# Late merges on GpSimd and the second expert bias as 12-row products, in a fused attention and mixture-of-experts kernel

## What is computed

```python
x = x + tanh(g_xattn[0]) * cross_attention(layernorm(x), ctx)          # 16 heads of 16
x = x + tanh(g_ffn[0]) * ffn(layernorm(x))

def ffn(hidden):
    a = attention(layernorm(hidden) * ln1_w + ln1_b)  # 16 heads of 128, causal, rope, biases
    h = hidden + a
    return h + moe(layernorm(h) * ln2_w + ln2_b)

def moe(h):                                           # 1024 tokens, E = 4 experts, I = 256
    raw = softmax(h @ w_gate)
    top_vals, top_idx = top_k(raw, 2)
    w = softmax(top_vals)                             # two gates a token
    comb = zeros((t, E)).at[arange(t)[:, None], top_idx].add(w)
    hmid = gelu(einsum('td,edi->tei', h, we1) + be1)
    eout = einsum('tei,eid->ted', hmid, we2) + be2    # be2: 4 x 256, the second expert bias
    return einsum('te,ted->td', comb, eout)
```

## Time and profile before

| | us |
|---|---|
| median of 3 runs | 463.28 |
| lowest and highest run | 463.11, 465.21 |
| profiled execution | 467.53 |
| its span | 465.70 |
| granted TensorE clock over the span | 0.983 of full |

### The profile page before, as it was taken

The page is one execution under the profiler, slowest core; times in us unless marked ns, Lnnn a source line. Parts: engine busy times, 40 slices in busy tenths (PEclk is TensorE's granted clock), DMA queues, the critical chain, the costliest instruction groups (busy, mean ns, idle before and its releaser), DMA issues.

```text
span 465.7 us, 10305 instructions
## 1 busy us (share of the span) xinstructions
PE 415.1 (89%) x3135; PEld 361.4 (78%) x3150; DVE 364.4 (78%) x1124; ACT 286.3 (61%) x655; POOL 301.2 (65%) x433
## 2 busy tenths in 40 slices
PE   0477997998899899999999999999999996598994
PEld 0366876886776799899899898998998986586994
DVE  3854568677789797897798788888888877928997
ACT  3357674755235777587677677677677675375440
POOL 5898959720598487587587687677677555343551
PEclk9999999999999899999999999999999998989998
DMA  5600000200256875775865865855955655000011
GB/s 153 189 3 2 1 3 2 92 2 1 46 113 125 174 149 119 174 150 108 203 143 106 189 136 118 196 131 108 225 119 109 145 80 112 4 0 2 1 45 45
DMA packets 71795, 44.53 MB, mean 96 GB/s; under 512 B 57424, under 2 KB 60112, under 8 KB 71760
## 3 DMA queue, kind: packets, MB, share of 16 engines
q1 hardware_dynamic: 67680, 35.42, 36.1%
q10 hardware_dynamic: 4080, 8.69, 6.5%
HBM read 13.68 MB, written 1.05 MB: 32 GB/s over the span
## 4 chain that ended last, share of the span: by engine, by line
PE 68%; DVE 17%; issue 5%; ACT 4%; POOL 3%; DMA 2%; ACTq 0%; SPq 0%; DVEq 0%; POOLq 0%
PE bank L1464 36%; PE bank L1532 5%; PE bank L1582 5%; DVE yacc L1309 3%; PE bank L1531 3%; PE bank L1583 3%; DVE yacc L1318 2%; PE bank L1404 2%; PE bank L1445 2%; POOL room L523 2%; PE bank L1359 2%; PE bank L1380 2%; PE bank L1405 1%; DMA qk_room<-qk_room 1%; PE bank L1426 1%
## 5 line engine op out<-in xcount | busy, mean ns | idle before, releaser
L799 ACT ACTIVATE probs<-sm,nm 128x128 f32<-128x128 f32 (+1 forms) x128 | 57.0, 447 | 44.1 <-DVE nm L1184 43.8
L789 ACT ACTIVATE probs<-turned 128x768 uint16<-128x768 uint16 x60 | 64.7, 1078 | 18.1 <-DMA turned<-halves 16.5
L1464 PE MATMUL bank<-hH,qk_parts 128*128 128x512 f32 x240 | 75.4, 395 | 0.0
L536 POOL COPY halves<-probs 128x768 uint16<-128x768 uint16 x64 | 52.6, 822 | 33.0 <-DVE probs L1208 31.1
L523 POOL TENSOR_TENSOR room<-room,qk_room 128x512 f32<-128x512 f32 x32 | 41.2, 1290 | 35.6 <-DMA qk_room<-qk_room 30.6
L1464 PE MATMUL bank<-hL,qk_parts 128*128 128x512 f32 x120 | 57.7, 481 | 0.9 <-DVE room L1105 0.9
L1464 PEld LDWEIGHTS bank<-hH,qk_parts 128*128 128x128 f32 x240 | 45.2, 188 | 9.5
L1105 DVE SCALAR_TENSOR_TENSOR room<-bank,qk_bias,cst_sb 128x512 f32<-128x512 f32 x64 | 47.5, 742 | 0.0
L1076 DVE TENSOR_REDUCE nxm<-bank 128x2 bf16<-128x512 f32 (+1 forms) x48 | 32.8, 688 | 18.1 <-PE bank L1405 17.5
L523 POOL TENSOR_TENSOR room<-room,q_room 128x512 f32<-128x512 f32 x32 | 41.1, 1287 | 5.5 <-DMA q_room<-q_room 5.5
L684 ACT ACTIVATE probs<-bank 128x512 f32<-128x512 f32 x48 | 28.3, 595 | 25.4 <-PE bank L1421 14.4
(11 more groups left out here) (241 smaller groups left out, 1291.8 us busy)
## 6 DMA issues: line engine op xcount, KB each, us to landing
qk_room<-qk_room SPq DMA_DIRECT2D x64, 128.0 KB, 2.4
q_room<-q_room SPq DMA_DIRECT2D x64, 128.0 KB, 2.4
stg<-in_wqkv ACTq DMA_DIRECT2D x6, 768.0 KB, 5.8
stge<-in_we ACTq DMA_DIRECT2D x7, 256.0 KB, 3.1
stg<-in_wqkv SPq DMA_DIRECT2D x2, 768.0 KB, 5.2
stgo<-in_wo ACTq DMA_DIRECT2D x6, 256.0 KB, 3.4
x_sb<-in_x SPq DMA_DIRECT2D x4, 256.0 KB, 4.1
turned<-halves SPq DMA_TRANSPOSE x64, 2.8
```

Of the source, the lines that this page charges most:

```text
L536: pool.tensor_copy(halves[:, j % 2, :, :], PR[:, j % 2, 0:384].bitcast(U16).rearrange("p (n h) -> p h n", h=2)).then_inc(s["b_split"], 1)
L789: act.activation(*merged(j - 3), ACT.Copy).then_inc(s["b_merge"], 1)
L799: ins = act.activation(PR[:, q, a:e], sm[:, q, a:e], ACT.Exp, bias=nm[:, q, t:t + 1], scale=-1.0, accum_out=rs[:, q, t:t + 1])
L1464: ins = pe.matmul(outp, l, r, start=(m == 0), stop=(m == n - 1))
```

## The change

1. **Late merges.** LATE falls from NU - 4 to NU - 9: merges of units 55 to 59 are made on POOL, in step T as merge(T-3) behind split(T), and ACT no longer makes them. The merged probabilities get four slots in place of two, so that merge(u) waits for PV(u-4) and no longer PV(u-2). From step 58 on, DVE makes maxima(T+1) ahead of normalise(T). At the end DVE's and ACT's order changes a little: each o_low moves a place ahead, and second_norm's phases 4 and 5 of the first two sequences come behind the last o_low; o_high(58) stands between the last two exponentials.
2. **Hidden low parts.** hidden_low2(0) and (1) are made on DVE, behind the statistics of the second half of second_norm, and no longer on POOL.
3. **Gates.** The turns of the logits stand between the two halves of expert_out(0). DVE makes `y * g + x` (residual_form) at the start, for sequences 0 and 1 ahead of the copy of the logits' turns, for 2 and 3 later. The second gate exponential becomes a Tanh, which stands behind Gelu and GH of middle(4); the gates are multiplied by g as they are formed, so that nothing is left to multiply at the end.
4. **Second bias.** The bias goes through PE: be2 is loaded four times three times onto 12 rows in each quarter of the partitions (12 transfers of 4x256 on SP, ahead of the second weight load), POOL turns it into high and low rows by five operations in units 16 to 20 (`bias_rows`), with two small reductions on DVE for the factors. The gates are packed in the same way (high, low, high; three DVE operations), turned on PE (`pack_turn`) ahead of expert_out(2), copied to wvL's first half, and `second_bias(c)` makes four products of 12 rows for each chunk, behind middle(8) and middle(12). `add_biases` adds them from PSUM, four operations of 128x512. The 32 operations L1309, the four L1325 and the transfer of be2 to 128 rows go. SP's output waits for the last accumulation.

The diff, cut to its core:

```diff
-        PTs = probs[:, 2:4, :]
+        PTs = probs[:, 2:6, :]
...
-        LATE = NU - 4
+        LATE = NU - 9
...
+            sp.wait_ge(s["q_parts"], 2 * B)
+            for q in range(4):
+                for r in range(3):
+                    row = 32 * q + E * r
+                    sp.dma_start(be2_raw[row:row + E, :], be2).then_inc(s["d_be"], 16)
...
# POOL
-                pool.wait_ge(s["b_pv"], u - 1)
+                pool.wait_ge(s["b_pv"], u - 3)
...
+            def bias_rows(n):
+                if n == 0:
+                    ins = pool.tensor_copy(be2_high.bitcast(F32R), be2_raw)
+                if n == 1:
+                    ins = pool.tensor_tensor(be2_low, be2_raw, be2_high, ALU.subtract)
+                if n == 2:
+                    ins = pool.tensor_scalar(be2_low, be2_low, small[:, 142:143], None, ALU.mult)
+                if n == 3:
+                    ins = pool.tensor_scalar(be2_raw, be2_high, small[:, 143:144], None, ALU.mult)
+                if n == 4:
+                    ins = pool.tensor_tensor(be2_parts[:, :], be2_raw, be2_low, ALU.add)
...
+                if i == 2 and j < 5:
+                    bias_rows(j)
+                if U * i + j - 3 >= LATE:
+                    merge(U * i + j - 3)
...
-            hidden_low2(0)
-            hidden_low2(1)
...
# ACT
-                if unit(i, j, 3):
+                if unit(i, j, 3) and not (isinstance(i, int) and U * i + j - 3 >= LATE):
                     merge(i, j)
...
-            merge(NP - 1, 6)
             exponentials(NP - 1, 6)
+            o_high(NP - 1, 6)
             exponentials(NP - 1, 7)
-            o_high(NP - 1, 6)
...
+                if n == 5:
                     act.wait_ge(s["c_gdiff"], 1)
-                    act.activation(gate[:, 400:408], gate[:, 392:400], ACT.Exp).then_inc(s["c_gexp"], 1)
+                    act.activation(gate[:, 400:408], gate[:, 392:400], ACT.Tanh, scale=-0.5).then_inc(s["c_gexp"], 1)
...
# DVE
+                if isinstance(i, int) and T >= AHEAD:
+                    maxima(*divmod(T + 1, U))
...
+            second_norm(2, 0, 2)
...
+            hidden_low2(0)
+            hidden_low2(1)
...
+            def residual_form(b):
+                y = yacc[:, 2 * b:2 * b + 2, :].rearrange("p t n -> p (t n)")
+                xb = x_sb[:, 2 * b:2 * b + 2, :].rearrange("p t n -> p (t n)")
+                dve.scalar_tensor_tensor(y, y, small[:, 97:98], xb, ALU.mult, ALU.add).then_inc(s["c_res"], 1)
+            residual_form(0)
+            residual_form(1)
...
-            link(dve.tensor_scalar(Gt(248, 8), Gt(400, 8), 1.0, None, ALU.add))
-            link(dve.reciprocal(Gt(256, 8), Gt(248, 8)))
-            link(dve.tensor_tensor(Gt(264, 8), Gt(256, 8), Gt(400, 8), ALU.mult))
+            dve.tensor_scalar(Gt(256, 8), Gt(400, 8), half_g, half_g, ALU.mult, ALU.add)
+            link(dve.tensor_scalar(Gt(264, 8), Gt(400, 8), minus_half_g, half_g, ALU.mult, ALU.add))
...
+            link(dve.tensor_copy(packed[:, :, :, 0:E].bitcast(F32R), gates))
+            dve.tensor_copy(packed[:, :, :, 2 * E:3 * E], packed[:, :, :, 0:E])
+            dve.tensor_tensor(packed[:, :, :, E:2 * E].bitcast(F32R), gates, packed[:, :, :, 0:E], ALU.subtract).then_inc(s["c_pack"], 1)
...
-                        ins = dve.scalar_tensor_tensor(yacc[:, n, :], be2_rows[:, e, :], gate[:, 4 * n + e:4 * n + e + 1], yacc[:, n, :],
-                                                       ALU.mult, ALU.add)
...
-                        dve.scalar_tensor_tensor(y, y, small[:, 97:98], xb, ALU.mult, ALU.add).then_inc(s["c_fin"], 1)
...
+                    dve.tensor_tensor(y, y, bank[4 + hf][:, :], ALU.add).then_inc(s["c_badd"], 1)
...
+            accumulate(0)
+            accumulate(1)
+            dve.wait_ge(s["c_pack_pe"], 1)
+            dve.tensor_copy(gates_turned, bank[4][:, 0:256]).then_inc(s["c_gT"], 1)
+            residual_form(2)
+            residual_form(3)
+            add_biases(0)
...
# PE
+            def second_bias(c):
+                for hf in range(2):
+                    rows_ = slice(32 * (2 * c + hf), 32 * (2 * c + hf) + 3 * E)
+                    for t in range(2):
+                        ins = pe.matmul(bank[4 + hf][:, 256 * t:256 * (t + 1)], gates_turned[rows_, t * P:(t + 1) * P], be2_parts[rows_, :],
+                                        start=True, stop=True)
...
+            expert_out(0, (0,))
             pe.wait_ge(s["c_lgT"], 1)
...
+            expert_out(0, (1,))
             expert_out(1)
...
+            middle(7)
+            pack_turn()
+            expert_out(2)
+            for n in range(8, 2 * NE):
                 middle(n)
+                if n == 8:
+                    second_bias(0)
+                if n == 12:
+                    second_bias(1)
```

More of the change, by code:

```diff
@@ L592, in _ @@
             split(NP - 1, 6)
+            merge(NU - 5)
+            split(NP - 1, 7)
             merge(NU - 4)
-            split(NP - 1, 7)
             merge(NU - 3)
@@ L1192, in _ @@
             dve.wait_ge(s["yacc_init"], B)
+            by_quad = ident.rearrange("p (q w) -> p q w", q=4)
+            dve.tensor_reduce(small[:, 143:144], by_quad[:, :, 0:2 * E], AX.XY, ALU.add)
+            dve.tensor_reduce(small[:, 142:143], by_quad[:, :, 2 * E:3 * E], AX.XY, ALU.add).then_inc(s["c_half"], 1)
             def output_add(m, b):
@@ L1212, in step @@
                 q = j % 2
-                if unit(i, j, 0) and not (isinstance(i, int) and T == 0):
+                if unit(i, j, 0) and not (isinstance(i, int) and (T == 0 or T > AHEAD)):
                     maxima(i, j)
+                if isinstance(i, int) and T >= AHEAD:
+                    maxima(*divmod(T + 1, U))
                 c, g = chunk_at(j)
@@ L1252, in _, with hidden_low2 @@
             output_add(LAST + 3, 3)
-            for phase in range(6):
+            second_norm(2, 0, 2)
+            def hidden_low2(b):
+                dve.wait_ge(s["c_hH"], b + 1)
+                cut = slice(256 * b, 256 * (b + 1))
+                dve.tensor_tensor(hL[:, :, cut], h2T[:, :, cut], hH[:, :, cut].bitcast(F32), ALU.subtract).then_inc(s["c_h"], 1)
+            hidden_low2(0)
+            hidden_low2(1)
+            for phase in range(1, 6):
                 second_norm(2, phase, 2)
@@ L1296, in _, with accumulate @@
             link(dve.tensor_tensor(Gt(0, 32), Gt(120, 32), Gt(152, 32), ALU.add))
-            dve.wait_ge(s["d_be"], 16)
-            dve.wait_ge(s["b_yadd"], NU // 2)
-            for m in range(2 * E):
+            packed = nh[:, 1, :].rearrange("p (t b w) -> p b t w", t=2, w=32)
+            gates = gate[:, 0:32].rearrange("p (b t e) -> p b t e", b=B, e=E)
+            link(dve.tensor_copy(packed[:, :, :, 0:E].bitcast(F32R), gates))
+            dve.tensor_copy(packed[:, :, :, 2 * E:3 * E], packed[:, :, :, 0:E])
+            dve.tensor_tensor(packed[:, :, :, E:2 * E].bitcast(F32R), gates, packed[:, :, :, 0:E], ALU.subtract).then_inc(s["c_pack"], 1)
+            def accumulate(m):
                 c, e = divmod(m, E)
@@ L1320, in _, with add_biases @@
                     ins.then_inc(s["c_acc"], 1)
[L1321 to L1325 removed]
+            def add_biases(c):
+                dve.wait_ge(s["c_be"], c + 1)
+                for hf in range(2):
+                    b = 2 * c + hf
+                    dve.wait_ge(s["c_acc"], 2 * (E * c + 1) + hf + 1)
+                    y = yacc[:, 2 * b:2 * b + 2, :].rearrange("p t n -> p (t n)")
+                    dve.tensor_tensor(y, y, bank[4 + hf][:, :], ALU.add).then_inc(s["c_badd"], 1)
[6 more added lines that the diff above has]
+            add_biases(0)
+            accumulate(2)
+            accumulate(3)
+            accumulate(4)
+            accumulate(5)
+            add_biases(1)
+            for m in range(6, 2 * E):
+                accumulate(m)
         @block.tensor
@@ L1636, in expert_out @@
                     pe.wait_ge(s["b_yadd"], NU // 2)
-                for hf in range(2):
+                for hf in parts:
                     if m >= 2:
```

77 lines of the change are left out of this document (46 added, 31 removed).

## The result

The changed kernel is slower: 474.70 us median of 4 runs (474.07 to 475.79) against 464.25 for before beside it (4 runs, 463.11 to 465.66), a ratio of 1.023 with a 95% interval of 1.0201 to 1.026. Measured again beside 23 runs of before it was 1.0157 (1.0104 to 1.021). The mean of all eight runs of the changed kernel is 474.3 us, against 466.0 for the 61 runs of before beside the first two groups of experiments (463.1 to 469.6), so that I work with **+8.4 us**; the four runs measured again lie 8.3 above the 23 of before beside them. The forecast was +3.05, as 466.3 us. Of the runs that follow, one of before at 699.25 us and one of "Tanh earlier" at 475.06 us count as slow and are in no mean and no ratio.

What follows compares the result with a forecast made beforehand. TensorE, busy 89%, was taken to bound the kernel, with VectorE ending it 3.83 us later. Late units 2.0, second norm 0.2, early part 0, gates through end 0.85 sum to +3.05 on 463.28: 466.3 us, 8-in-10 range 461.0 to 469.8.

Steps and rivals of the forecast that it cites:

- one fall was a rival: Gates: clock falls behind PE's pause of about 2 us ahead of expert_out(2), adding 1.5: 467.8 us; chance 0.15.
- What bounds the kernel, and the frame: Whole kernel: TensorE, busy 89%, bounds it; differences added in the 467.53 us profile are put on the median 463.28.
- Late units, +2.0: 375 to 404 us: merges behind splits delay PV(55) by 2.65 us; last o_low 400.5 plus 1.5 for the clock's fall.
- my upper bound of +3.2: Late units: cost if the clock falls at both pauses, ahead of PV(58) and of PV(60).
- Second norm, +0.2: Ahead of the experts: hidden_low2(0) on VectorE ends at 405.65, two moved phases cost 0.3; between -0.3 and +0.6.
- Early part, 0: Before the late units: bias loads, five GpSimd operations and two VectorE reductions cost nothing; upper end +2.7.
- Gates, expert_out(2) at 433.3: Gates: three of eight small VectorE operations held by GpSimd; expert_out(2) at 433.3 against 430.65, between 430.0 and 435.5.
- the upper end: Gates: every product with two SBUF inputs waits for a full subtraction; expert_out(2) comes 2.2 us later than taken.
- Second bias and the end, +0.85: End: two bias blocks of 0.6 us on PE, VectorE's tail shrinks by 2.8; VectorE ends at 464.05 against 463.20.
- 28.5 us of PE: From expert_out(2) to PE's end: work taken from before, added to 433.3 with 1.2 for bias, giving 463.0.
- The rivals: Gates slip through, 0.16; late units break even, 0.22; clock falls behind gates' pause, 0.15; products or GpSimd rows cost most, 0.05.
- The last rival's 470: Bias products or rows on GpSimd cost their upper ends, +1.8 and +2.7 on top, 470 us; chance 0.05.

Runs made afterwards that it cites:

- first two groups of experiments: Follow-up kernels run beside before, each group on a different chip; before had means of 466.5 and 465.6 us there.
- Tanh earlier: Changed kernel with Tanh ahead of Gelu of middle(4), as the only move; mean of nine runs 469.3 us, ratio to before 1.0075.
- both moves with the late units of before: Changed kernel, residual forms 0 and 1 behind gate difference, Tanh ahead of middle(4)'s Gelu, late units as in before; mean 464.8 us, ratio to before 0.9979.
- Merge ahead of split: Changed kernel, residual forms 0, 1 behind gate difference, Tanh ahead of middle(4)'s Gelu, GpSimd's late merges ahead of splits; mean 463.0 us, ratio to before 0.9937.
- Order on VectorE alone: Changed kernel, residual forms 0, 1 behind gate difference, Tanh ahead of middle(4)'s Gelu, merges and ScalarE's end as before; mean 463.4 us, ratio to before 0.9947.
- two runs of before named above: Two runs of the unchanged kernel: 463.11 us with a mean granted clock of 0.998 over the span, 468.82 us with 0.983.
- both moves at the gates: Changed kernel with residual forms 0 and 1 behind the gate difference and Tanh ahead of middle(4)'s Gelu; mean 467.5 us, ratio to before 1.0013.
- one merge less: Changed kernel, residual forms 0, 1 behind gate difference, Tanh ahead of middle(4)'s Gelu, merge(55) left on ScalarE; mean 465.2 us, ratio to before 0.9982.

## Why the prediction was wrong

The direction and the places were right, the size was not: +3.05 forecast, +8.4 measured, and the range ended at 469.8. Two steps failed. In the gates the forecast let three small operations be held where four were, had Tanh end 1.0 us too early, and its sum put nothing for a fall of the clock behind either of the two pauses there (one fall was a rival). In the late units it took one fall of the clock, as before, where most profiles have two. Besides, the sum was put on a median that was too low.

- **What bounds the kernel, and the frame.** I put a sum made in one profiled execution on the median of three runs. That median, 463.28, was 2.7 us below the mean of 61 runs. This alone moves the forecast to 469.0. The profiled execution of 467.53 should have warned me: it lies outside the three runs (463.11 to 465.21), and the row with 0.91 from 140 to 160 us was to be seen.
- **Late units, +2.0.** Single events came as worked out: PV(55) 378.52 (forecast 378.6), PV(58) 388.20 (388.7), PV(60) 393.21 (393.6), last o_low 402.07 (400.5 and 1.5 for the fall). But the last o_low's +2.03 flatters the forecast: before had lost 0.8 us by PV(53) through its early fall. From PV(53) on it is 33.1 against 30.25, +2.8, and by many runs +3.6 (+2.9 by the ratio). The step that failed is the size of the clock's part: I took the fall as alike in both. The four profiles with the late units of before (before twice, the change without late units, both moves with the late units of before) have one fall each between 374 and 404 us and 29.6 to 30.3 us from PV(53) to the last o_low. Of the seven with all five merges behind the splits, two have one fall and 32.5 to 33.1 us, five have two and 33.9 to 34.8 us. So an equal fall leaves +2.8, and a second one, which my upper bound of +3.2 had allowed for, adds about 1.4. That the merges' place behind the splits is the cause was right ("Merge ahead of split"). VectorE's new order, which I gave no price of its own, is no loss ("Order on VectorE alone").
- **Second norm, +0.2.** +0.43 by the traces (first expert product 6.28 us behind the last o_low, before 5.85). hidden_low2 on VectorE takes 0.69 us, and the two moved phases put it later.
- **Early part, 0.** Nothing to be seen in the windows up to 360 us.
- **Gates, expert_out(2) at 433.3.** This is the term that failed most. The 433.3 stands in the frame of before, without the delay of the late units: 27.4 us behind the first expert product. It came 29.9 us behind it (438.26 - 408.35; before 24.8), so that the wait and the operations took 2.5 us more than forecast. The wait ahead of expert_out(1) grew by 0.7, less than I gave (1.0 to 1.5), but I priced no fall behind it, since 1.39 us had had none; behind 2.13 there was one, 1.5 us. It pushed middle(4), and Tanh stands behind middle(4)'s Gelu: Tanh ended 23.4 us behind the first expert product instead of 22.4. Then every second one of the dependent operations was held for a whole subtraction, four and not three: 5.6 us where I had 3.9. The sentence from the Trainium skill ("SBUF — State Buffer", "SBUF: two separate sides": an exclusive lock for a whole instruction) gave the upper end. The measurement agrees with the lock, four operations at 1.14 to 1.26 us beside subtractions of 1.3, none over 0.3 where GpSimd had nothing to do; but only each second operation met it, not every one, as that upper end had assumed.
- **Second bias and the end, +0.85.** The products were 0.6 us a block as taken (from the last product of middle(8) at 443.82 to the second of middle(9) at 444.92 there are 1.10 us, where two steps of 0.23 are usual). Of the 1.8 us more that the draining of "TensorEngine Tiling (Array Packing)", "Key Properties", in the Trainium skill might have cost, there is no sign. VectorE ends 0.91 behind PE (forecast 1.07). (A middle is 6 products, not 12 as the description of the kernel says; its duration in the sum came from the rows.) What failed was the 28.5 us of PE: expert_out(2) ran at half clock, +1.46. In the two profiles the forecast missed 7.38 - 3.05 = 4.3 us, and 2.5 of them lie in the gates and 1.5 here.
- **The rivals.** The fall behind the gates' pause was a rival with a chance of 0.15 and happened in every profile with that pause. I treated the rivals as excluding one another and the forecast; gates late, falls at two places and the low base came together. (The last rival's 470 is 466.3 + 1.8 + 2.7 = 470.8.) As a sum of its parts, 463.28 + 2.7 (base) + 3.6 (late) + 4.0 (gates and bias) = 473.6, it is the measured mean to within 1 us. How much of it is the clock can be estimated: the eight runs of the change have a mean granted clock of 0.982, those of before 0.990, and the two runs of before named above differ by 5.7 us for 0.015, which makes about 3 of the 8.4 us.

## What to carry to other kernels

Where an engine's queue gets extra work for a unit that is older, put it ahead of the newer unit's work: the same merges cost 3 to 4 us behind the splits and nothing that could be measured ahead of them. A chain of small dependent operations on VectorE belongs where GpSimd is idle; the same eight operations took 5.6 us beside GpSimd's subtractions and 1.55 ahead of them. And a sum that is made in one profile is to be put on a mean of many runs, with every pause that the change adds priced with the fall of the clock behind it.

## What the hardware showed that I had not expected

- At the gates the granted clock fell to 1.2 GHz for 3 to 4 us (in one profile for nearly 7) behind each pause of TensorE of 2.12 to 2.13 us (four profiles) and of 2.93 to 2.95 us (four profiles), and not behind pauses of 0.98 and of 1.39 to 1.43. It isn't the length of the pause alone. In the late units of the change it stayed at 2.4 GHz behind 3.26 us in one profile and fell behind 3.16 in the other, and it fell behind 1.90. Ahead of the experts a pause of 3.17 to 3.20 us was followed by a fall in six profiles and by none in three (both moves at the gates, order on VectorE alone, one merge less), which held 1.00 from 404 to 420 us. 20 products that nobody reads, put into the pause ahead of expert_out(2), kept it at 2.4 GHz.
- VectorE and GpSimd took turns one for one: with both queues full, each second dependent operation of 128x8 or 128x32 lasted 1.14 to 1.26 us, the next one 0.18 to 0.28.
- Four products with 12 rows on the input side cost 0.6 us with what they take from the products around them.
